# A diffusion block with routed experts: per-head values with Wv and weighing in quarters of the array, in place of the folded product Wv Wo

## The reference, cut to what matters

```python
q = (xq @ wq).reshape(b, sq, H, DH).transpose(0, 2, 1, 3)
k = (ctx @ wk).reshape(b, sk, H, DH).transpose(0, 2, 1, 3)
v = (ctx @ wv).reshape(b, sk, H, DH).transpose(0, 2, 1, 3)
attn = softmax(einsum('bhqd,bhkd->bhqk', q, k) / sqrt(DH))
out = einsum('bhqk,bhkd->bhqd', attn, v)
return out.transpose(0, 2, 1, 3).reshape(b, sq, INNER) @ wo + bo
```

## Time and profile before

| | us |
|---|---|
| median of 3 runs | 2113.37 (2111.95 to 2113.82) |
| the profiled execution, its span | 2124.9 |
| TensorE busy in it | 2039.6 (96%) |
| ScalarE, VectorE, GpSimd busy | 1386.2, 1323.4, 1071.9 |

### The profile page before, as it was taken

How to read it: one execution, slowest core, us unless ns; L and a number is a source line. 1 busy time by engine, 2 the same in 40 slices (tenths; PEclk the granted TensorE clock), 3 DMA queues, 4 the chain that set the end, 5 groups by cost and what they waited for, 6 DMA issues and landing times. The chain is left out here.

```text
span 2124.9 us, 38735 instructions
## 1 busy us (share of the span) xinstructions
PE 2039.6 (96%) x11068; PEld 1337.7 (63%) x11068; DVE 1323.4 (62%) x3389; ACT 1386.2 (65%) x2659; POOL 1071.9 (50%) x1198
## 2 busy tenths in 40 slices
PE   7899999999999999999999999999999889899996
PEld 5455555555555555555555565555555558799996
DVE  5554657676767676767676666666656545455565
ACT  4566666676667676767676767676766666566663
POOL 2444444636363637363737373737363445556664
PEclk9999999999999999999999999999999999999998
DMA  4110111121111111111111111111122312222256
GB/s 153 45 26 25 50 35 51 46 50 45 49 45 50 46 53 45 49 45 49 45 49 45 49 45 51 47 48 52 44 54 64 96 48 57 58 56 72 60 185 215
DMA packets 136321, 127.35 MB, mean 60 GB/s; under 512 B 14665, under 2 KB 110569, under 8 KB 136234
## 3 DMA queue, kind: packets, MB, share of 16 engines
q1 hardware_dynamic: 127466, 109.11, 18.7%
q0 software_dynamic: 8768, 17.20, 2.5%
HBM read 86.63 MB, written 40.67 MB: 60 GB/s over the span
## 5 line engine op out<-in xcount | busy, mean ns | idle before, releaser
L1928 POOL TENSOR_TENSOR pr<-pr,sm 128x512 f32<-128x512 f32 x256 | 277.7, 1098 | 483.7 <-DVE sm L1462 483.7
L1126 ACT ACTIVATE kp<-ps 128x512 f32<-128x512 f32 x512 | 298.9, 601 | 179.5 <-PE ps L283 176.2
L834 PE MATMUL ps<-tt,V 128*128 128x512 f32 x768 | 380.3, 593 | 3.5 <-ACT tt L1126 3.5
L1452 DVE TENSOR_REDUCE mx<-ps 128x8 f32<-128x512 f32 x256 | 176.8, 691 | 306.3 <-PE ps L783 306.3
L1126 ACT ACTIVATE tt<-ps 128x512 f32<-128x512 f32 x512 | 275.2, 591 | 40.2 <-PE ps L813 39.6
L783 PE MATMUL ps<-kp,hf 128*64 128x256 f32 x2048 | 276.8, 392 | 6.9 <-DVE pr L1455 3.9
L283 PE MATMUL ps<-cT,M 128*128 128x512 f32 x768 | 262.0, 464 | 0.0
L783 PEld LDWEIGHTS ps<-kp,hf 128*64 128x64 f32 x2048 | 124.4, 136 | 196.9 <-DVE pr L1455 142.4
L1126 ACT ACTIVATE pt<-ps 128x512 f32<-128x512 f32 x256 | 153.6, 600 | 141.4 <-PE ps L795 139.1
L283 PE MATMUL ps<-hk,M 128*128 128x512 f32 x768 | 242.2, 438 | 0.0
L941 PE MATMUL ps<-xT,wt 128*128 128x128 f32 (+1 forms) x1728 | 221.9, 278 | 4.0 <-DVE wt L1753 4.0
(11 more groups left out here) (235 smaller groups left out, 3470.3 us busy)
## 6 DMA issues: line engine op xcount, KB each, us to landing
mod<-emb_s SPq DMA_DIRECT2D x96, 256.0 KB, 4.3
xr<-rows_s SPq DMA_DIRECT2D x144, 66.0 KB
cb<-y_s SPq DMA_DIRECT2D x32, 256.0 KB
x_in<-in_x_dram SPq DMA_DIRECT2D x16, 256.0 KB, 4.4
xn_s<-x_in SPq DMA_DIRECT2D x16, 256.0 KB, 2.1
res<-xn_s SPq DMA_DIRECT2D x16, 256.0 KB, 2.8
c_in<-in_ctx_dram SPq DMA_DIRECT2D x16, 256.0 KB, 4.7
y_s<-res SPq DMA_DIRECT2D x16, 256.0 KB, 2.0
```

Source lines behind the costliest of these rows:

```text
L834: mm = nc.tensor.matmul(psO[:], Vw[a][:, g * HG + head_at(h), :], tt[:, h, :], start=(g == 0 and h == 0), stop=ends)
L1126: return nc.scalar.activation(o, i, ACT.Copy)
L1452: nc.vector.tensor_reduce(mx[:, p % 2, :], heads(psS[p % 2][:]), AX_X, ALU.max).then_inc(max_done, 1)
L1928: tensor(v, v, sm[:, p, :].unsqueeze(2).broadcast_to([P, HG, 64]), ALU.mult).then_inc(prob_done, 1)
```

## The change

Wv and Wo stay apart. Setup computes M only; Wv is split in a high and a low part (`split_values`), Wo is loaded as it is. Each slot now computes the values of its unit, one token tile at a time, with three float32r matmuls of 512 columns (`values`), emptied by ScalarE. The weighing is then 64x64: for each tile, head and sequence one matmul of 64 rows, 64 weights and 64 columns; the sequence (e) selects the row half and the bank, the head's parity the column half. The sums of the even sequences are copied by ScalarE, those of the odd ones by VectorE (`weighed_out`), which also copies the turned probabilities of tiles 1 and 3. The projection multiplies them by Wo, with the tokens in the output's partitions: 16 matmuls of 128 columns per unit, into `psO`. The splits of heads, the biased outputs in ScalarE and the turns back of both attention sums go; GpSimd adds the bias to the residual beforehand (`add_bias`), in the new tiles `y1r` and `y2r`.

The stages are grouped: all four turns, the weighing in two halves, all four scores, the projection, four values, eight keys. The banks are dealt out anew.

```diff
+            def values(i, u, t, bank):
+                a, g = divmod(u, 2)
+                src = hk if a == 0 else cT
+                mm3(bank[:], lambda k: src[:, k, t * P:(t + 1) * P], lambda k: WV[a][:, k, g * CT:(g + 1) * CT]).then_inc(v_done, 1)
...
+            def weigh(i, u, pair):
+                if pair == 0:
+                    pe.wait_ge(vp_done, v_count(i, u, NT - 1))
+                    wait(turned(i, u, 0))
+                    wait(turned(i, u, 1))
+                else:
+                    for w in left_in(i, u, WEIGHED[3]):
+                        wait(w)
+                for t in range(NT):
+                    if pair == 0 and t > 1:
+                        wait(turned(i, u, t))
+                    if t == 0 or pair == 0 and t > 1:
+                        pe.sem_inc(seen, 1)
+                    for j in range(2):
+                        for odd in range(2):
+                            h = 4 * pair + 2 * j + odd
+                            g, c = divmod(h, HH)
+                            for e in range(2):
+                                keep = slice(64 * e, 64 * e + 64)
+                                mm = nc.tensor.matmul(WEIGHED[2 * pair + e][64 * odd:64 * odd + 64, 256 * j + 64 * t:256 * j + 64 * t + 64], vp[keep, t, 64 * h:64 * h + 64],
+                                                      pt[keep, t, c * P + 64 * g:c * P + 64 * g + 64], start=True, stop=True)
+                mm.then_inc(w_done, 1)
...
-                    mm = nc.tensor.matmul(psO[:], Vw[a][:, g * HG + head_at(h), :], tt[:, h, :], start=(g == 0 and h == 0), stop=ends)
+                if j % 2 == 0:
+                    wait(weighed(i, u, j))
+                    wait(weighed(i, u, j + 1))
+                for t in range(NT):
+                    mm = nc.tensor.matmul(psO[:, t * D:(t + 1) * D], os[:, j, t * P:(t + 1) * P], WO[a][:, HH * g + j, :],
+                                          start=(g == 0 and j == 0 and t == 0), stop=(g == 1 and j == HH - 1 and t == NT - 1))
...
+                if last:
+                    for pair in range(2):
+                        weigh(li, lu, pair)
+                if here:
+                    for p in range(NT):
                         scores(i, u, p)
...
                 if last:
+                    for j in range(HH):
+                        project(li, lu, j)
...
+                if here:
+                    for t in range(NT):
+                        product("v", t)
...
+            def turn_out(i, u, p):
+                dve.wait_ge(T_done, 4 * seq(i, u) + p + 1)
+                nc.vector.tensor_copy(pt[:, p, :], TURNED[p][:]).then_inc(pt_dve, 1)
+
+            def weighed_out(i, u, pair):
+                dve.wait_ge(w_done, 2 * seq(i, u) + pair + 1)
+                nc.vector.tensor_copy(half_sums(pair, 1), WEIGHED[2 * pair + 1][:].rearrange("p (j t q) -> p j t q", j=2, t=NT)).then_inc(os_dve, 1)
...
+                if last:
+                    for p in (1, 3):
+                        turn_out(li, lu, p)
+                    for pair in range(2):
+                        weighed_out(li, lu, pair)
                 for p in range(NT):
...
+                hooks = {0: ((1, 2, after_attn2), (5, 1, context), (7, 3, after_glu)),
+                         1: ((4, 2, stats3), (6, 2, norm3), (8, -1, ln1_stats)),
+                         2: ((1, 0, after_attn1), (2, 3, router_sum), (4, 3, router_dot), (3, 2, lambda c: ln_lo(c, 2)), (4, -1, ln1), (6, 2, lambda c: c_last(c) or glu_mul(c, 0)), (7, 2, lambda c: c_last(c) or glu_split_lo(c, 0)), (8, -1, lambda c: ln_lo(c, 0)), (8, 3, top_first)),
+                         3: ((0, 3, top_second), (1, 3, counts), (4, 0, stats2), (place_at(i - 3)[1], 3, place_out), (6, 3, gates), (7, 0, norm2))}[u]
...
+            def add_bias(c, a):
...
+                tensor(row[:], row[:], b_o[:, a, :].unsqueeze(1).broadcast_to([P, NT, D]), ALU.add).then_inc(bias_done[a], 1)
```

More of the change, by code:

```diff
@@ L756, in wait, with keys @@
                 pe.wait_ge(*w)
-            def keys(i, u, h):
+            def keys(i, u, h, bank):
                 a, g = divmod(u, 2)
@@ L777, in scores @@
                         pe.wait_ge(hx_hi[1], i)
-                if not (isinstance(n, int) and n < 2):
-                    pe.wait_ge(sub_done, n - 1)
+                elif live(*before(i, u)):
+                    wait(weighed(*before(i, u), p - 1))
+                bank = SCORED[p][:].rearrange("p (c s k) -> p c s k", c=HH, s=2)
                 for s in range(2):
                     cols = slice(p * P + 64 * s, p * P + 64 * s + 64)
-                    for j in range(2):
-                        mm = nc.tensor.matmul(psS[p % 2][64 * j:64 * j + 64, :].rearrange("p (h s k) -> p h s k", h=HH, s=2)[:, :, s, :],
-                                              hf[u // 2][:, cols], kp[:, j * HH:(j + 1) * HH, cols], start=True, stop=True)
-                        if s == 1:
-                            mm.then_inc(s_done, 1)
@@ L875, in place @@
             def place(c):
-                bank = place_bank(c)[0]
+                bank = psM
                 pe.wait_ge(rk, RS * c + 16)
@@ L1005, in next_key @@
-                def next_key(h):
-                    if h < len(RINGS[u]):
-                        bank = RINGS[u][h]
-                        if last:
-                            for w in [(pt_done, 4 * seq(li, lu) + 4)] if bank is psT else [] if bank in psS else t_free(li, lu, 3 if bank is psH else 2):
-                                wait(w)
-                        if here and bank in psS:
-                            pe.wait_ge(sub_done, 4 * seq(i, u) + 4)
-                    keys(*after(i, u), h)
@@ new lines, in slot, with product @@
+                if last:
+                    for pair in range(2):
+                        weigh(li, lu, pair)
+                if here:
+                    for p in range(NT):
+                        scores(i, u, p)
+                if last:
+                    for j in range(HH):
+                        project(li, lu, j)
+                def product(kind, x):
+                    made, banks = products(i, u), RINGS[u]
+                    j = made.index((kind, x))
+                    bank = banks[j % len(banks)]
+                    if j >= len(banks):
+                        for w in emptied(i, u, *made[j - len(banks)]):
+                            wait(w)
+                    elif bank in SCORED and here:
+                        pe.wait_ge(sub_done, 4 * seq(i, u) + SCORED.index(bank) + 1)
+                    elif bank in psS and isinstance(i, int) and i == NC:
+                        pe.wait_ge(eu_act, 3 * E)
+                    elif bank is psF and u < 2 and ok(i - 3):
+                        pe.wait_ge(f2_out, i - 2)
+                    if kind == "v":
+                        values(i, u, x, bank)
+                    else:
+                        keys(*after(i, u), x, bank)
```

542 lines of the change are left out of this document (192 added, 350 removed).

## The result

The changed kernel is slower: 2170.63 us (median; 2163.93 to 2173.62) against 2113.6 for the kernel before (2111.95 to 2113.9), a ratio of 1.027 with a 95% interval of 1.0252 to 1.0289. The forecast was 1970 us and its range 1880 to 2062. The profiled execution took 2169.7 us; that of before took 2124.9.

The account below looks back on a forecast made before the run. TensorE's summed work was taken as the bound. A round of 104.9 us was to become 92.3 of work plus 4.0 of stalls, 96.3; sixteen rounds gain 138 us, setup 5, so 2113.4 becomes 1970 us, range 1880 to 2062.

Parts of the forecast that it names:

- 83.5 us, plus 4W: TensorE's work in a round of four slots after the change: 83.5 us without the weighing, plus four times W.
- W: TensorE's time for the new 64x64 weighing in one slot, 128 records: forecast 2.2 us, four quarters at a time.
- B in its first form: Rival: only two quarters of the array work at once; 101.9 us a round, 2060 us; chance 0.18 for both forms.
- C: Rival: quarters of the array don't overlap at all, weighing 7.1 us per slot; 2238 us; chance 0.06.
- D: Rival: TensorE takes records no faster than a fixed rate, 0.085 us each, however small; 2462 us; chance 0.07.
- E: Rival: weight loads of 0.053 us aren't hidden where quarters share rows, weighing 4.4 us per slot; 2111 us; chance 0.05.
- two rules of the Trainium skill: On TensorE: about 62 ns per matmul under one way of decoding; weight loads overlap running matmuls only where row groups differ.
- Sum 4.0: TensorE's stalls in a round, mostly behind VectorE's queued work: 4.0 us over four slots, between 0 and about 8.
- Other costs I set at nothing: ScalarE, GpSimd, SP's transfers, the banks of the values and TensorE's clock: no time added to a round.
- TensorE's clock: the stalls are shorter: 2.61 idle us in a stretch left TensorE's clock at 1.00 and the new stalls are shorter: no cost.
- Setup: -5 forecast: Setup ahead of the rounds: 12 tiles go, two splits of Wv come; net -5 us, between 0 and -9.
- 16 rounds x: Gain over the chunks' rounds: 16 times 104.9 less 96.3 us, 138 us in all.

Follow-up runs that it names:

- e5: The kernel of e3 with TensorE's loop over rounds written out as in e1; 2072.68 us, 0.9715 of the kernel before.
- e10: The kernel of e5 with the first quarter's scores between the two halves of the weighing; 2080.0 us, 0.9763 of the kernel before.
- e3: The changed kernel with first statistics, first expert pick and hk's split moved from ahead of the copies of turned quarters; 2107.71 us, 0.9902 of the kernel before.
- e12: The changed kernel itself, measured again; 2209.54 us, 1.0356 of the kernel before.
- e13: The kernel of e5 with a round's last statistics behind VectorE's copies and the fourth norm one quarter later; 2063.21 us, 0.9658 of the kernel before.
- e2: The kernel before with two rounds instead of one in TensorE's loop body; 2132.17 us, 0.9995 of the kernel before.
- e7: The kernel of e3 with half of the weighing's matmuls left out, body 1732 instructions; 0.9506 of the kernel before.
- e1: The changed kernel with TensorE's loop over rounds 4 to 14 written out, other engines' loops kept; 2172.43 us, 1.0183 of the kernel before.
- e8: The kernel of e3 with three quarters of the weighing's matmuls left out, body 1476 instructions; 0.9326 of the kernel before.
- e6: The kernel of e3 with TensorE's loop turned by two slots, its body beginning with a round's third slot; 2086.43 us, 0.9782 of the kernel before.
- e11: The kernel of e10 with a round's last statistics behind VectorE's copies and the fourth norm one quarter later; 2068.87 us, 0.972 of the kernel before.
- e4: The changed kernel with all four copies of the turned quarters on ScalarE; 2125.41 us, 0.9954 of the kernel before.

## Why the prediction missed

**The work was right.** The step "83.5 us, plus 4W" with W = 2.2 forecast 92.3 us. W measured 2.02, scores 3.60 (3.5 and a change of shape), projection 3.60 (3.57), values 2.90 (2.8). The round less its gaps is 93.2 in e5 (100.7 - 7.5; the profile's idle time gives 94.5) and 93.8 in e10 (101.5 - 7.7), where hardly any half clock blurs it: about 1 to 2 us more than forecast. Rivals B in its first form, C, D and E are out: 64 x 64 matmuls in four quarters run at once, and 128 of them with their loads take 2.02 us, 0.016 us each. Of the two rules of the Trainium skill in the prediction (TensorE: Matmul & The Clock Gate, Parts 1 and 3), neither price shows here: 0.016 us is a quarter of the first, and the loads are hidden even where quarters share their rows.

**VectorE's and ScalarE's load was right in the main.** 77.73 us of VectorE in the round shown (77.5 forecast), 63.87 of ScalarE (about 59).

**The stalls were mis-sized, and this is the step that failed first.** "Sum 4.0" was 17.4. Each wait for the copies by slot, forecast and measured:
- Slot 3: forecast 2, measured 2.85. The mechanism, the rest of hk and the first pick ahead of the copies, is the one seen at 1015.19 to 1016.90.
- Slot 2: forecast 0.7, measured 2.65. The tail of the first statistics holds two operations that take 1.1 us instead of 0.17 beside GpSimd. Less their excess, 1.9 us, the wait would be about the 0.7 forecast, an estimate. The trace of the kernel before has the same two at the same place, behind TensorE's full queue, so they could have been read there:

```profile
1062.73 1.18 DVE L1480 TENSOR_SCALAR lv<-lv 128x4 f32<-128x4 f32 x1
...
1064.01 1.14 DVE L1483 TENSOR_TENSOR lv<-lv 128x4 f32<-128x4 f32 x1
```

- Slot 1: forecast 0.3, measured 1.15. Slot 0: forecast 0.7; no wait for these copies there, since the gap at the branch lies ahead and hides it.
- The gated unit and the third turn: forecast 0.3 at one place, measured 4.3 with all small gaps. This part was not taken away by any run.
- The branch and the gaps inside the weighing, 5.9 us: absent. The step "Other costs I set at nothing" went through ScalarE, GpSimd, SP, the banks and the clock, and not through TensorE's own instructions, though the prediction itself counted 128 new records and as many loads per slot. The trace of before had the row for it, three reads in 1100 us, and I didn't ask what would make it grow.

**"TensorE's clock: the stalls are shorter" was wrong.** The row of 2.61 idle us at 1.00 was one gap, and one gap is no rule: of the gaps of 2.5 us and more in ten rounds of the changed kernel, seven left the clock alone as well and 21 didn't. Nor were the stalls shorter, but 2.6 to 2.9 us in one piece, and the clock is 0.5 for 3.4 or 6.8 us behind them. It makes a long stall dearer, by up to 2.6 us as read at 1129.45: against the first profile, e3 took away 5.8 us of gaps and the round fell by 7.9. This term, set at nothing, was some 4 us a round.

**Outside the rounds.** Setup: -5 forecast. The first turn of a slot starts at 58.41 us and before at 54.35, so setup is 4.1 longer; why wasn't tried. The first rounds, lighter and without long gaps, bring it back by the first place (373.3 against 378.2). "16 rounds x" counted the rounds at the ends as full ones. In the first profile the rest did gain 30 us, in e12 nothing, so this term stays between 0 and 30 us where I had 43.

**The sum.** With the waits for VectorE's copies and the gap at the branch removed (e13) the change is worth -3.4%; at 2113 us that is 2041, inside the range. The forecast would have needed the last 2.1 and 4.1 us of gaps to go as well. Rival D set a price on every record; none named the reading of the loop's instructions or the clock, and so the range ended under the result.

## What to carry to other kernels

When a change takes work from the engine that is the bound, ask what had been hidden behind that engine's full queue: here the tail of another engine's queue (in the kernel before) and a sequencer that waits for 3.4 to 3.9 us at a branch for instruction reads (in e2) cost nothing while TensorE's queue was full. Once it ran empty, gaps and clock together cost some 19 us a round. Count the instructions of a loop body as one counts bytes of a buffer: matmuls in quarters of the array are nearly free in time and cost two instructions each. A copy that the bounding engine waits for goes ahead of everything in its engine's queue that has a later user.

## What the runs showed of the hardware

- TensorE kept a loop body of 1136 or 1476 instructions, read one of 2244 or 2264 again in every pass, and did either with one of 1732 (e7: read in seven passes of ten, kept in three). A read is 16 KB (2.87 MB in 175) and takes about 1 us. At a branch to code not held the branch record lasts 3.3 to 3.9 us, in e7 4.6 to 5.2; to code held, 0.2. The Trainium skill (Advanced Engine Details and Errata, "ISA Cache") gives TensorE 128 KB in lines of 16 KB or 256 instructions, which is 2048 instructions. The size of a read agrees with the trace, and so do the bodies over 2048 and the one of 1476; that 1732 were read again in seven passes doesn't follow from it, nor that a pass makes more reads than its body has lines (9 for 1732 instructions, 11 for 2244). No run shows why.
- Written-out code is read without a gap at e1's round ends. In the dense stretch of 63 records a us gaps of 1.9 to 2.1 us a round stayed in e5 and e13, about half of them without a read near.
- Weighing in four quarters of the array: 128 records of 64 x 64 x 64 float32 and 128 loads in 2.02 us.
- VectorE's TENSOR_TENSOR and TENSOR_SCALAR operations on four columns take 1.1 to 1.2 us instead of 0.17 when they fall beside a GpSimd operation on a 128x512 tile, in both kernels; a TENSOR_REDUCE to four columns stayed at 0.19 beside one.
- The granted clock fell to its lower level behind gaps of 1.9 to 3.1 us, not behind each of them (seven of 2.5 to 3.0 in the changed kernel had none behind). e8 and e10, whose gaps are all under 1.5 us, had no half clock in ten rounds. But the length of one gap isn't the whole: e5, e6, e7, e11 and e13 had nine stretches of it (3.4 us each) without such a gap, each right behind a weighing torn by three gaps of 0.2 to 0.45 us, and e4 had four with no gap over 1.4 us ahead.
